# Two layers in fp32 on one core: the last expert slot's rows go to their tokens by a permutation product instead of through memory

## The chip, the cores and the metric

The kernel is written in Bass, with queues and semaphores set by hand, and runs on one core of one Trainium2 chip. The metric is the device time of one execution in microseconds, the median of several runs.

## What is computed

Eight tiles of 128 tokens, 256 wide (`x`, 1024 rows), go through two layers in fp32. Layer 0 is a cross attention with 16 heads of 16 and then a routed feed-forward with 8 experts; layer 1 is a cross attention with normed queries and keys, then a causal self attention of 16 heads of 128 and a second mixture of experts. This case concerns the passage from layer 0's experts to layer 1's cross attention:

```python
# layer 0, feed-forward: each token goes to its best expert only
route = sigmoid(h @ router_w); max_ind = argmax(route, 1); max_prob = its value
for e in range(8):
    out = out + where(max_ind == e, (silu(h @ gate_w[e]) * (h @ up_w[e])) @ down_w[e], 0)
x = x + tanh(g_ffn[0]) * out * max_prob
# layer 1, cross attention; its keys and values come from the context, not from x
q = rms_norm(layernorm(x) @ q_w.T + q_b) * norm_q_w
k = rms_norm(ctx @ k_img_w.T + k_img_b) * norm_k_img_w
v = ctx @ v_img_w.T + v_img_b
x = x + tanh(g_xattn[1]) * (attention(q, k, v) @ o_w.T + o_b)
```

## The kernel before, in words

**Slots.** The tokens are sorted by expert. `place` and `posf`/`pos` hold for each token its row in a list of 15 slots of 128 rows (`SLOTS`); a slot belongs to one expert. GpSimd scatters the normalised rows to `xs_d` in memory at these places (L1740), and each engine runs `slots`, which calls its `tile(j, ...)` for j = 0 to 14. In a slot TensorE turns the rows (L1453), makes gate and up products in three parts of split precision (`up`, L1461 to L1467), turns the hidden rows of the slot before (L1474) and multiplies them by the down weights (L1482). VectorE copies the result to `y_s` (`output_rows`, L1680), and SP stores it to `ys_d` (`store`, L1781).

**The passage.** When all 15 stores have landed, GpSimd gathers the rows of tile b back from `ys_d` into `FX` (eight indirect DMAs, L1765), and VectorE adds them to `X`, scaled by `rmax` (`add_experts`, L1604), and takes statistics (L1605, `moments` L841 to L843). GpSimd raises the variance to the power -1/2 (`power`, L800); VectorE makes the first two normalised tiles `xn` (`ln_scale`, L846). TensorE turns them (L453), ScalarE copies them to `xT` (`columns`, L671), TensorE makes the queries (L465), ScalarE their scaled form `qT` and squares (L689, L690), and then scores follow (L500).

**What stands beside it.** Keys and values of layer 1 are made from the context: `keys_values(i)` on TensorE (L1426) and VectorE (L1666, L1667, L783), six tiles early and the last two (`MOST` to `B`) after the last slot. `normalise_keys` (L1598) scales them. Each normalised key tile in `K1` is turned on TensorE (L1523) and copied back by ScalarE (`key_columns`, L1537). ScalarE makes the masked form `k2T` for the first two tiles (L711) and loads the table for Exp (L715); GpSimd makes it for the others (`masked_keys`, L984). `fill` (L347) issues products of zeros. SP then loads the first weights of the self attention (L2090, L2094) once the last down product is done.

**The attention's steps.** `xattn_*(.., 1)` runs steps n = -3 to 8. VectorE's step n has the two halves of softmax of tile n + 1 (`softmax`, L864 and L865, 128 by 1024 each), the mean of queries (L874), and the normalisation of the context of tile n (L869, L870), which TensorE turns in the next step (L453 on `x_cx`). At n = -1 stands `rest_of_rows()`. The order on every engine is the order of the calls; an engine waits at an instruction for its semaphores, with all that is behind it.

Constants: `B` 8, `EARLY` 4, `MOST` 6, `FIRST` 2. `KEYS` is [4, 5, 6, 7, 0, 1, 2, 3], the order in which key tiles are made.

## Time and profile before

| | us |
|---|---|
| median of 3 runs (lowest, highest) | 761.36 (760.95, 764.85) |
| profiled execution, its own time | 763.18 |
| its span, first to last instruction | 761.5 |
| TensorE busy | 728.8 |
| VectorE, ScalarE, GpSimd busy | 455.1, 374.2, 297.0 |
| chain that ended last: TensorE's share | 81% |
| mean granted clock of TensorE | 0.988 |

The span is cut up by what the engines do: layer 0's cross attention to about 87 us, its routing and slots to 189, the passage to about 206, layer 1's cross attention to about 282, then self attention and the second mixture.
### The profile page before, as it was taken

To read this page: it belongs to the slowest core of one execution; us is meant where nothing else is said; L and a number is where in the kernel's file an instruction comes from. 1 tells how busy PE (TensorE), PEld (TensorE's weight loads), DVE (VectorE), ACT (ScalarE), POOL (GpSimd) and SP (SyncE) were. 2 spreads that over 40 slices of the span, in tenths; PEclk is the share of its full clock that TensorE was granted. 3 is DMA by queue.
4 is the path that set the end of the run, shared out by engine and by line. 5 is a ranking of instruction groups with operands and counts; after the bars stand their busy time and mean duration, and the time that the engine had idled before them with its cause. 6 is when DMAs were issued, how large, how long until landed. Compare 5 with 4: busy or idle time off the path is not lost.

```text
span 761.5 us, 14062 instructions
## 1 busy us (share of the span) xinstructions
PE 728.8 (96%) x4683; PEld 611.3 (80%) x4684; DVE 455.1 (60%) x823; ACT 374.2 (49%) x876; POOL 297.0 (39%) x376
## 2 busy tenths in 40 slices
PE   7999989999889989999999999999999999999998
PEld 6887657887567767898899988998778888888886
DVE  6888587554687854345444554355555665665665
ACT  4888236664377754445445454445442323323323
POOL 3233265664655656422232123212324434434430
PEclk9999999999799999999999999999999999999999
DMA  8980121111300011010110101200004343343321
GB/s 286 418 329 2 28 83 36 55 41 35 118 2 1 2 36 36 22 35 22 36 55 21 34 21 46 72 1 22 22 25 129 114 121 100 121 116 99 122 95 56
DMA packets 24745, 57.40 MB, mean 75 GB/s; under 512 B 3568, under 2 KB 13296, under 8 KB 23680
## 3 DMA queue, kind: packets, MB, share of 16 engines
q1 hardware_dynamic: 23936, 54.77, 22.0%
q0 software_dynamic: 768, 2.10, 0.9%
q8 instruction: 25, 0.41, 0.2%
q14 instruction: 16, 0.13, 0.1%
HBM read 50.76 MB, written 6.09 MB: 75 GB/s over the span
## 4 chain that ended last, share of the span: by engine, by line
PE 81%; DVE 7%; ACT 6%; POOL 2%; DMA 2%; issue 1%; DVEq 0%; SPq 0%; ACTq 0%; POOLq 0%
PE PS L351 16%; PE PS L353 16%; PE PS L352 16%; PE PS L1824 7%; PE PS L1482 4%; PE PS L465 3%; PE PS L500 2%; PE PS L509 2%; PE PS L471 2%; PE PS L1830 2%; PE PS L1467 2%; PE PS L1464 2%; PE PS L1461 2%; PE PS L522 1%; POOL Z L846 1%
## 5 line engine op out<-in xcount | busy, mean ns | idle before, releaser
L1250 ACT ACTIVATE hhh<-hh 128x512 fp32r<-128x512 f32 x50 | 31.6, 632 | 104.6 <-DVE hh L1276 94.7
L351 PE MATMUL PS<-tTh,wh 128*128 128x512 f32 x200 | 78.3, 392 | 0.8 <-DVE tTl L661 0.5
L353 PE MATMUL PS<-tTh,wl 128*128 128x512 f32 x200 | 77.9, 389 | 0.0
L352 PE MATMUL PS<-tTl,wh 128*128 128x512 f32 x200 | 77.8, 389 | 0.0
L661 DVE TENSOR_TENSOR hhl<-hh,hhh 128x512 fp32r<-128x512 f32 x50 | 52.3, 1047 | 35.4 <-ACT hhh L1250 35.4
L1342 POOL CAST wh<-wraw 128x512 fp32r<-128x512 f32 (+1 forms) x50 | 26.1, 523 | 109.9 <-PE PS L353 109.9
L2038 POOL CAST ah<-araw 128x512 fp32r<-128x512 f32 (+1 forms) x32 | 16.2, 506 | 134.6 <-PE PS L353 134.6
L1935 ACT ACTIVATE sm<-sm,nmx 128x128 f32<-128x128 f32 x128 | 49.7, 390 | 37.7 <-DVE nmx L1998 37.7
L661 DVE TENSOR_TENSOR oTl<-PS,oTh 128x512 fp32r<-128x512 f32 x32 | 22.1, 691 | 71.5 <-ACT oTh L1929 71.5
L1344 POOL TENSOR_TENSOR wl<-wraw,wh 128x512 fp32r<-128x512 f32 (+1 forms) x50 | 58.0, 1160 | 8.4 <-POOL wh L1342 7.9
L1531 POOL TENSOR_TENSOR wgl<-WE,wgh 128x512 fp32r<-128x512 f32 x28 | 46.9, 1696 | 26.4 <-ACT wgh L1577 25.8
L351 PE MATMUL PS<-tTh,ah 128*128 128x512 f32 x128 | 53.0, 414 | 1.7 <-DVE tTl L834 1.5
L1272 DVE TENSOR_TENSOR act_s<-act_s,PS 128x512 f32<-128x512 f32 x44 | 30.2, 687 | 38.4 <-PE PS L353 38.4
L353 PE MATMUL PS<-tTh,al 128*128 128x512 f32 x128 | 50.2, 393 | 0.0
L352 PE MATMUL PS<-tTl,ah 128*128 128x512 f32 x128 | 49.9, 390 | 0.0
L1239 ACT ACTIVATE act_s<-PS 128x512 f32<-128x512 f32 x50 | 29.9, 599 | 32.0 <-PE PS L353 32.0
L351 PEld LDWEIGHTS PS<-tTh,wh 128*128 128x128 f32 x200 | 37.5, 188 | 9.9 <-issue 1.1
L353 PEld LDWEIGHTS PS<-tTh,wl 128*128 128x128 f32 x200 | 37.5, 188 | 7.9
L352 PEld LDWEIGHTS PS<-tTl,wh 128*128 128x128 f32 x200 | 37.5, 188 | 7.5
L864 DVE TENSOR_REDUCE x_mx<-PS 128x8 f32<-128x1024 f32 x32 | 38.9, 1217 | 5.7 <-PE PS L500 5.7
L1929 ACT ACTIVATE pT<-PS 128x512 f32<-128x512 f32 x32 | 17.6, 596 | 49.7 <-PE PS L1830 49.6
L865 DVE TENSOR_TENSOR x_prob<-PS,x_mx 128x1024 f32<-128x1024 f32 x32 | 39.2, 1224 | 1.1
(276 smaller groups left out, 1985.4 us busy)
## 6 DMA issues: line engine op xcount, KB each, us to landing
WE<-moe SPq DMA_DIRECT2D x8, 1536.0 KB, 18.1
wraw<-moe SPq DMA_DIRECT2D x25, 384.0 KB, 3.0
araw<-attn SPq DMA_DIRECT2D x16, 384.0 KB
cwb<-cw_d SPq DMA_DIRECT2D x20, 256.0 KB, 3.9
WX<-wx SPq DMA_DIRECT2D x4, 512.0 KB, 7.2
avraw<-attn_v SPq DMA_DIRECT2D x8, 256.0 KB
xs_d<-zeros SPq DMA_DIRECT2D x1, 1920.0 KB, 22.2
ys_d<-y_s SPq DMA_DIRECT2D x15, 128.0 KB, 1.7
```

The costliest lines, as they stand in the source:

```text
L351: nc.tensor.matmul(out, wh_, xh_, start=first, stop=False, **kw)
L352: nc.tensor.matmul(out, wh_, xl_, start=False, stop=False, **kw)
L353: return nc.tensor.matmul(out, wl_, xh_, start=False, stop=last, **kw)
L661: return nc.vector.tensor_tensor(lo, src, hi.bitcast(F32), ALU.subtract)
L864: ch.link(nc.vector.tensor_reduce(m8, sc, AX.X, ALU.max))
L865: nc.vector.tensor_tensor(m_.prob[b % 2][:, 8 * g:8 * g + 8, :], sc, m8.unsqueeze(2).broadcast_to([P, 8, S]), ALU.subtract).then_inc(s.sub ...
L1250: nc.scalar.activation(hhh[half][:, :], hh[half][:, :], ACT.Copy).then_inc(s.hi_done, 1)
L1344: nc.gpsimd.tensor_tensor(wl[par][:, a0:a1], wraw[par][:, a0:a1], wh[par][:, a0:a1].bitcast(F32), ALU.subtract).then_inc(s.w_split, 1)
L1482: m = nc.tensor.matmul(PS[:, 6 + par, 0:D], hT[:, k, :], w[:, k, :], start=(k == 0), stop=(k == I0 // P - 1))
L1531: eng.tensor_tensor(wgl[mat][:, c, :], expert_columns(e, mat, c), wgh[mat][:, c, :].bitcast(F32), ALU.subtract).then_inc(done, 1)
L1824: m = nc.tensor.matmul(PS[:, si % 4, t * S:(t + 1) * S], lhs[:, a0:a0 + S], rhs[:, a0:a0 + S], start=True, stop=True)
L1935: nc.scalar.activation(sm[:, b, :], sm[:, b, :], ACT.Exp, bias=nmx[:, b:b + 1], scale=AD ** -0.5, accum_out=sums[:, b:b + 1]).then_inc(aex ...
```

## The change

Slot 14's rows no longer go through memory. `ys_d`'s last slot is filled with zeros at the start, SP no longer stores slot 14, and GpSimd's gathers wait for slots 0 to 13 alone. For the tokens in slot 14 a permutation is made: SP writes the positions `posf` to `pos_d` in memory and reads them back to all partitions into `last_perm`, the free half of `rT`; one VectorE operation after slot 2 compares them with the rows of the last slot. TensorE multiplies `y_s[0]` by it for each tile (`last_product`) and adds the gathered rows of tiles 0 to 3 by a product with the identity in the same PSUM bank (`gathered_rows`). For tiles 4 to 7 ScalarE copies the product to `last_rows`, the space of `gs`, and VectorE adds it and the gathered rows one after the other, two tiles in step n = -1 and two in step n = 0. The key tiles are turned back in another order and in other banks (`TURNED`, `TURN_BANKS`), the last two (`LATE_KEYS`) in the attention's step n = -1; the fillers are fewer.

```diff
+LATE_KEYS = KEYS[B - 2:]
+TURNED = [4, 5, 0, 1, 2, 3]
+TURN_BANKS = [1, 3, 0, 2, 7, 6]
...
+        last_perm = rT[:, :, (B - CTX) * S:]
+        last_rows = gs2[:, :, :].rearrange("p a (k d) -> p (a k) d", d=D)
...
             # scores(b) on TensorE
+                if L and b == 0:
+                    pe.wait_ge(Es.k1_ready, 2)
+                    pe.wait_ge(Es.last_read, 2)
...
-            pe.wait_ge(Es.kt_free, B)
-            fill(4, 7)
+            pe.wait_ge(Es.kt_free, len(TURNED))
+            fill(2, 7)
...
+                if n == -1:
+                    pe.wait_ge(Es.k1_ready, 2)
+                    for b in LATE_KEYS:
+                        rows_to_columns("KT", b, K1[:, b, :])
...
-                key_columns(act, MOST, B)
...
-                if n == -1:
-                    rest_of_rows()
+                if n in (-1, 0):
+                    rest_of_rows(EARLY + 2 * n + 2)
...
+            def keys_back(k):
+                i, out = TURNED[k], PS[:, TURN_BANKS[k], :]
+                pe.wait_ge(s.k1_ready, 1)
+                for c in range(C):
+                    m = nc.tensor.transpose(out[:, c * P:(c + 1) * P], K1[:, KEYS[i], c * P:(c + 1) * P], ident[:, :])
+                m.then_inc(s.kt_done, 1)
+            def last_product(b, signal=False):
+                if b in FIRST_OF_BANK:
+                    pe.wait_ge(s.kt_free, FIRST_OF_BANK.index(b) + 1)
+                m = nc.tensor.matmul(last_bank(b), last_perm[:, b // EARLY, b % EARLY * P:(b % EARLY + 1) * P], y_s[0][:, :], start=(b in FIRST_OF_BANK), stop=signal, skip_group_check=True)
+                if signal:
+                    m.then_inc(s.last_done, 1)
+            def gathered_rows(b):
+                pe.wait_ge(s.gathered[b], 16)
+                if b >= FIRST:
+                    pe.wait_ge(s.place_read, b)
+                nc.tensor.matmul(last_bank(b), ident[:, :], FX[:, b, :], start=False, stop=True, skip_group_check=True).then_inc(s.last_done, 1)
             turn_hidden(SLOTS - 1)
+            keys_back(0)
+            keys_back(1)
             down(SLOTS - 1, (SLOTS - 1) % 2)
+            keys_back(2)
+            keys_back(3)
+            pe.wait_ge(s.perm_done, 2)
+            pe.wait_ge(s.y_ready, SLOTS)
+            for b in (0, 2, 1, 3):
+                last_product(b)
+            gathered_rows(0)
+            gathered_rows(1)
             for i in range(MOST, B):
                 keys_values(i)
-            for i in range(B):
-                if i == MOST:
-                    pe.wait_ge(s.kt_free, 3)
-                    fill(15, 2)
...
+            for b in range(EARLY, B):
+                last_product(b, b % 2 == 1)
+            keys_back(4)
+            keys_back(5)
+            gathered_rows(2)
+            gathered_rows(3)
...
             hidden_columns(SLOTS - 1)
-            key_columns(act, 0, MOST)
+            key_columns(act, 0, EARLY)
+            for k in range(2):
+                act.wait_ge(s.last_done, 3 + k)
+                nc.scalar.activation(gs2[:, k, :], PS[:, TURN_BANKS[2 + k], :], ACT.Copy).then_inc(s.last_read, 1)
+            key_columns(act, EARLY, len(TURNED))
...
             # add_experts(dve, ch, b); add(src) is the old operation with another source
+            if b < EARLY:
+                dve.wait_ge(Es.last_done, b + 1 if b < FIRST else b + 3)
+                add(last_bank(b)).then_inc(Es.place_read, 1)
+            else:
+                dve.wait_ge(Es.last_read, 2)
+                ch.link(add(last_rows[:, b - EARLY, :]))
+                dve.wait_ge(Es.gathered[b], 16)
+                ch.link(add(FX[:, b, :]))
...
+                if isinstance(j, int) and j == 2:
+                    dve.wait_ge(late_in, 64 + 16 * C)
+                    v.tensor_scalar(last_perm, last_perm, rows_after[:, :], float(SLOTS * P - 1), ALU.add, ALU.is_equal).then_inc(s.perm_done, 1)
...
             output_rows(SLOTS - 1, (SLOTS - 1) % 2, (SLOTS - 1) // 2)
+            for b in range(FIRST):
+                add_experts(dve, ch, b)
+            moments(ch, 0, FIRST)
             dve.wait_ge(s.kms_done, 1)
-            keys_values(MOST, B)
+            keys_values(MOST, MOST + 1, False)
+            powered(dve, "ln3")
+            for k in range(FIRST):
+                ln_scale(xb1.xn[k][:, :], X[:, k, :], k).then_inc(xs[1].ln_done, 1)
+            keys_values(MOST + 1, B)
+            for b in range(FIRST, EARLY):
+                add_experts(dve, ch, b)
+            moments(ch, FIRST, EARLY)
+            normalise_keys(dve, MOST, B, 2)
...
             for par in range(2):
-                pool.wait_ge(s.y_out[par], 16 * ((SLOTS + 1 - par) // 2))
+                pool.wait_ge(s.y_out[par], 16 * ((SLOTS - par) // 2))
             for b in range(B):
                 nc.gpsimd.indirect_dma_start(FX[:, b, :], None, ys_d, bass.IndirectOffsetOnAxis(pos[:, b:b + 1], 0)).then_inc(s.gathered[b], 16)
...
+                if b == MOST - 1:
                     power(pool, "ln3")
...
+            sp.dma_start(pos_d.rearrange("b p -> p b"), posf[:, :], allow_slow_non_contiguous=True).then_inc(late_in, 16)
+            sp.wait_ge(late_in, 64)
+            for c in range(C):
+                sp.dma_start(last_perm[:, c, :], pos_d[EARLY * c:EARLY * (c + 1), :].rearrange("b p -> (b p)").partition_broadcast(P)).then_inc(late_in, 16)
...
-            store(SLOTS - 1, (SLOTS - 1) % 2)
```

TensorE, from the last product of slot 14 (`WE,hT`) to the first scores, before (`WX,rT` are the last keys and values, `ident,K` the key transposes, `zeros` the fillers, `x_xn` the first normalised rows):

```order
L1482 MATMUL PS<-WE,hT 128x256
L1426 MATMUL PS<-WX,rT 128x512 x4
L1523 MATMUL PS<-ident,K 128x128 x12
L347 MATMUL PS<-zeros 128x512 x15
L1523 MATMUL PS<-ident,K 128x128 x4
L347 MATMUL PS<-zeros 128x512 x4
L453 MATMUL PS<-ident,x_xn 128x128 x2
L465 MATMUL PS<-x_xT,WX 128x128 x4
```

and with the change (`y_s,rT` is the product with the permutation, `FX,ident` the gathered rows):

```order
L1508 MATMUL PS<-WE,hT 128x256
L1540 MATMUL PS<-ident,K 128x128 x4
L1547 MATMUL PS<-y_s,rT 128x256 x4
L1557 MATMUL PS<-FX,ident 128x256 x2
L1452 MATMUL PS<-WX,rT 128x512 x4
L1547 MATMUL PS<-y_s,rT 128x256 x4
L1540 MATMUL PS<-ident,K 128x128 x4
L1557 MATMUL PS<-FX,ident 128x256 x2
L358 MATMUL PS<-zeros 128x512 x2
L464 MATMUL PS<-ident,x_xn 128x128 x2
L476 MATMUL PS<-x_xT,WX 128x128 x4
```

The keys and values of the last two tiles now stand behind six products, two of which wait for gathers.

ScalarE in the same place, before (`warm` is the one element that carries the table load):

```order
L1550 ACTIVATE hT<-PS 128x512 [waits e_ht_done] x2
L1537 ACTIVATE K<-PS 128x256 [waits e_kt_done] x6
L711 ACTIVATE x_k2T<-K,pair_rows 128x2x128 [waits e_kt_free,bias_done]
L711 ACTIVATE x_k2T<-K,pair_rows 128x2x128
L711 ACTIVATE x_k2T<-K,pair_rows 128x2x128 [waits e_kt_free]
L711 ACTIVATE x_k2T<-K,pair_rows 128x2x128
L1537 ACTIVATE K<-PS 128x256 [waits e_kt_done] x2
L715 ACT_TABLE_LOAD
L715 ACTIVATE warm<-mhalf 128x1
L671 ACTIVATE x_xT<-PS 128x256 [waits x1_turn_done]
```

and with the change:

```order
L1611 ACTIVATE hT<-PS 128x512 [waits e_ht_done] x2
L1598 ACTIVATE K<-PS 128x256 [waits e_kt_done] x4
L1651 ACTIVATE gs<-PS 128x512 [waits e_last_done] x2
L1598 ACTIVATE K<-PS 128x256 [waits e_kt_done] x2
L730 ACTIVATE x_k2T<-K,pair_rows 128x2x128 [waits e_kt_free,bias_done]
L730 ACTIVATE x_k2T<-K,pair_rows 128x2x128
L730 ACTIVATE x_k2T<-K,pair_rows 128x2x128 [waits e_kt_free]
L730 ACTIVATE x_k2T<-K,pair_rows 128x2x128
L733 ACT_TABLE_LOAD
L733 ACTIVATE warm<-mhalf 128x1
L690 ACTIVATE x_xT<-PS 128x256 [waits x1_turn_done]
```

The masked key tiles (`x_k2T`) stand behind two copies `gs<-PS` that wait for the products with the permutation, and the table load stands behind them.

VectorE with the change, from the first softmax to the second (`x_mx<-PS`, `x_prob` are one half of it):

```order
L885 TENSOR_REDUCE x_mx<-PS 128x8 [waits x1_scores_done]
L886 TENSOR_TENSOR x_prob<-PS,x_mx 128x1024 [waits dve_chain]
L1669 SCALAR_TENSOR_TENSOR X<-gs,rmax,X 128x256 [waits e_last_read]
L1669 SCALAR_TENSOR_TENSOR X<-FX,rmax,X 128x256 [waits e_gathered4,dve_chain]
L1680 BN_STATS st<-X 128x6 [waits dve_chain]
L1669 SCALAR_TENSOR_TENSOR X<-gs,rmax,X 128x256 [waits e_last_read]
L1669 SCALAR_TENSOR_TENSOR X<-FX,rmax,X 128x256 [waits e_gathered5,dve_chain]
L1680 BN_STATS st<-X 128x6 [waits dve_chain]
L862 BN_AGGR mv<-st 128x2 [waits dve_chain]
L862 BN_AGGR mv<-st 128x2
L864 TENSOR_SCALAR ms<-mv 128x2 [waits dve_chain]
L895 TENSOR_SCALAR q_mean<-PS 128x1 [waits x1_turn_done]
```

Before, this place had one addition (tile 7), its statistics and the moments of four tiles; the same seven rows of additions now stand after the second softmax as well.

## Rows read from the trace of the kernel before

**Rows 1.** The page, busy time of the engines (share of the span, instructions):

```profile
PE 728.8 (96%) x4683; PEld 611.3 (80%) x4684; DVE 455.1 (60%) x823; ACT 374.2 (49%) x876; POOL 297.0 (39%) x376
```

**Rows 2.** Chain of waits in order of time (start us, us, what), between the layers:

```profile
189.19 0.43 DVE y_s L1680
189.65 1.71 DMA ys_d<-y_s
191.63 4.15 DMA FX<-ys_d,pos
...
202.15 0.39 ACT x_xT L671
```

**Rows 3.** Timeline of TensorE (start us, us, line, what, count of records [idle before]):

```profile
87.99 3.26 PE L1426 MATMUL PS<-WX,x_cT 128*128 128x512 f32 x4
...
187.17 1.99 PE L1482 MATMUL PS<-WE,hT 128*128 x8 [0.79 <-ACT hT L1550]
188.99 3.60 PE L1426 MATMUL PS<-WX,rT 128*128 128x512 f32 x8
192.43 1.63 PE L1523 MATMUL PS<-ident,K 128*128 128x128 f32 x12
...
202.59 2.07 PE L465 MATMUL PS<-x_xT,WX 128*128 128x128 f32 x8 [0.47 <-ACT x_xT L671]
...
223.33 0.38 PE L453 MATMUL PS<-ident,x_cx 128*128 128x128 f32 x2
```

**Rows 4.** Timeline of ScalarE in the same stretch:

```profile
186.42 0.60 ACT L1550 ACTIVATE hT<-PS 128x512 f32<-128x512 f32 x1 [3.07 <-PE PS L1474]
...
194.44 1.74 ACT L711 ACTIVATE x_k2T<-K,pair_rows 128x256 f32<-128x256 f32 x4
199.39 0.66 ACT L1537 ACTIVATE K<-PS 128x256 f32<-128x256 f32 x2 [3.21 <-PE PS L1523]
200.07 1.28 ACT L715 ACT_TABLE_LOAD   x1
201.37 0.20 ACT L715 ACTIVATE warm<-mhalf 128x1 f32<-128x1 f32 x1
```

**Rows 5.** Stretches: us, busy by engine, granted clock, DMA share, GB/s:

```profile
192.00:194.00 2.00, 2.00 (x15) 1.50 (x14) 1.19 (x6) 1.16 (x5) 1.62 (x2) 1.00 1.02 355
...
202.00:204.00 2.00, 1.53 (x7) 1.41 (x7) 1.54 (x4) 0.38 (x1) 1.52 (x3) 0.50 0.24 66
```

**Rows 6.** Timeline of VectorE, end of the slots and first steps of attention:

```profile
185.98 0.42 DVE L1680 COPY y_s<-PS 128x256 f32<-128x256 f32 x1 [1.20 <-PE PS L1482]
...
200.96 0.73 DVE L846 TENSOR_SCALAR x_xn<-X,mv,rstd 128x256 f32<-128x256 f32 x2
...
213.05 0.47 DVE L1604 SCALAR_TENSOR_TENSOR X<-FX,rmax,X 128x256 f32<-128x256 f32 x1
...
214.51 0.15 DVE L874 TENSOR_SCALAR q_mean<-PS 128x1 f32<-128x1 f32 x1
...
220.62 0.16 DVE L874 TENSOR_SCALAR q_mean<-PS 128x1 f32<-128x1 f32 x1 [1.18 <-PE PS L488]
221.37 0.26 DVE L869 RECIPROCAL x_rden<-PS 128x16 f32<-128x16 f32 x1 [0.59 <-PE PS L529]
221.66 0.42 DVE L870 TENSOR_TENSOR x_cx<-PS,x_rden 128x256 f32<-128x256 f32 x1
```

**Rows 7.** GpSimd's timeline, second gather, and the gathers' landing (their line's view):

```profile
192.97 0.96 POOL L1765 DMA_INDIRECT FX<-ys_d,pos  x1 [0.30 <-issue]
...
DMA to landing us min/median/max: 2.7/2.8/2.8
```

**Rows 8.** VectorE's permutation, a load's landing, and SP's loads of slot rows:

```profile
94.66 1.22 DVE L1652 TENSOR_TENSOR gs<-PS,posf 128x1024 f32<-128x1024 f32 x1
...
rw<-rw SPq DMA_DIRECT2D x1, 16.0 KB, 6.5
...
L1777 SPq DMA_DIRECT2D xs_s<-xs_d x5: 327/340/425, 107.8 to 124.7; - x5
```

More of the change, by code:

```diff
@@ L170, in build @@
         pos = sb("pos", [P, B], mybir.dt.uint32, e)
+        rows_after = sb("rows_after", [P, 1], where=e)
+        last_perm = rT[:, :, (B - CTX) * S:]
+        last_rows = gs2[:, :, :].rearrange("p a (k d) -> p (a k) d", d=D)
         exf = sb("exf", [P, SLOTS], where=e)
@@ L316, in build @@
             xt_done, xt_ready, g_done, u_done, silu_done = (sem("e_" + k) for k in ("xt_done", "xt_ready", "g_done", "u_done", "silu_done"))
[L317 removed]
+            place_read, perm_done, h_ready, ht_done, ht_ready, d_done, y_ready = (sem("e_" + k) for k in ("place_read", "perm_done", "h_ready", "ht_done", "ht_ready", "d_done", "y_ready"))
             xt_low, w_high = sem("e_xt_low"), sem("e_w_high")
             w_low = [sem(f"e_w_low{i}") for i in range(2)]
+            last_done, last_read = sem("e_last_done"), sem("e_last_read")
             sums_done, experts_done, zeroed = sem("e_sums_done"), sem("e_experts_done"), sem("e_zeroed")
@@ L392, in second_turns @@
                     ("xT", n + 3, "A"), *(("F", b, "D") for b in ins), ("O", n - 1, "D"), ("oT", n, "A"),
-                    *([("Q2", n + 2, "D")] if n > -2 else []), ("cx", n, "D"),
+                    *([("Q2", n + 2, "D")] if n > -2 else []), ("cx", n, "D"), *([("KT", b, "A") for b in LATE_KEYS] if n == -1 else []),
                     *(("F", b, "D") for b in {B - 1: [4], B: [5, 6, 7]}.get(n, []))]
@@ L767, in xattn_act @@
                     columns("xT", n + 3, m_.xT)
+                if n == -1:
+                    for b in LATE_KEYS:
+                        copy("KT", b, K1[:, b, :], D)
                 if B - 4 <= n < B:
@@ L788, in build @@
         X_PARTS = [(0, FIRST), (FIRST, EARLY), (EARLY, B)]
-        POWERS = [("ln1", 0, FIRST), ("ln1", FIRST, EARLY), *(("ln1", b, b + 1) for b in range(EARLY, B)), ("ln2", 0, EARLY), ("ln2", EARLY, MOST), ("ln2", MOST, MOST + 1), ("ln2", MOST + 1, B), ("ln3", 0, FIRST), ("ln3", FIRST, EARLY), ("ln3", EARLY, B),
+        POWERS = [("ln1", 0, FIRST), ("ln1", FIRST, EARLY), *(("ln1", b, b + 1) for b in range(EARLY, B)), ("ln2", 0, EARLY), ("ln2", EARLY, MOST), ("ln2", MOST, MOST + 1), ("ln2", MOST + 1, B), ("ln3", 0, FIRST), ("ln3", FIRST, EARLY), ("ln3", EARLY, MOST), ("ln3", MOST, B),
                   ("ln4", 0, B)]
@@ L1006, in xattn_pool @@
                     routing_constants()
-                if L and n == 1:
-                    power(pool, "ln3", EARLY)
+                if L and n in (1, 3):
+                    power(pool, "ln3", EARLY + n - 1)
                 if n + 3 < B:
@@ L1427, in keys_values @@
                 m.then_inc(s.kv_done, 1)
-            nc.tensor.matmul(PS[:, 6, 0:P], ones[:, :], earlier[:, :], start=True, stop=True).then_inc(s.ids_done, 1)
+            nc.tensor.matmul(PS[:, 6, 0:P], ones[:, :], earlier[:, :], start=True, stop=True).then_inc(s.lg_done, 1)
             pe.wait_ge(wx_in[1][0], 16)
@@ L1513, in ffn_pe @@
+            pe.wait_ge(s.y_ready, SLOTS)
[3 more added lines that the diff above has]
+            gathered_rows(1)
             for i in range(MOST, B):
                 keys_values(i)
-            for i in range(B):
-                if i == MOST:
-                    pe.wait_ge(s.kt_free, 3)
-                    fill(15, 2)
-                pe.wait_ge(s.k1_ready, 1 if i < MOST else 2)
-                after(pe, s.kt_free, i - 3)
-                for c in range(C):
-                    m = nc.tensor.transpose(PS[:, i % 4, c * P:(c + 1) * P], K1[:, KEYS[i], c * P:(c + 1) * P], ident[:, :])
-                m.then_inc(s.kt_done, 1)
+            for b in range(EARLY, B):
+                last_product(b, b % 2 == 1)
@@ L1526, in expert_columns, with last_bank @@
+            keys_back(4)
+            keys_back(5)
+            gathered_rows(2)
+            gathered_rows(3)
+        FIRST_OF_BANK = [0, 1, EARLY, MOST]
+        def last_bank(b):
+            k, part = (b % FIRST, b // FIRST) if b < EARLY else (b // 2, b % 2)
+            return PS[:, TURN_BANKS[k], part * D:(part + 1) * D]
         def expert_columns(e, mat, c):
@@ L1619, in ffn_dve @@
             ch.link(v.memset(V1[:, :, :, XD:XD + 1], 1.0))
+            v.tensor_reduce(rows_after[:, :], earlier[:, :], AX.X, ALU.add)
             dve.wait_ge(s.ex_done, 1)
@@ L2213, in _, with more_rows @@
             ffn_dve(dve, ch)
-            for b in range(B - 1):
-                add_experts(dve, ch, b)
-                if b == FIRST - 1:
-                    moments(ch, 0, FIRST)
-                    normalise_keys(dve, MOST, B, 2)
-                if b == EARLY - 1:
-                    moments(ch, FIRST, EARLY)
-                    powered(dve, "ln3")
-                    for k in range(FIRST):
-                        ln_scale(xb1.xn[k][:, :], X[:, k, :], k).then_inc(xs[1].ln_done, 1)
-            def last_rows():
-                add_experts(dve, ch, B - 1)
-                moments(ch, EARLY, B)
-            xattn_dve(dve, 1, ch, last_rows)
+            def more_rows(b0):
+                for b in range(b0, b0 + 2):
+                    add_experts(dve, ch, b)
+                moments(ch, b0, b0 + 2)
+            xattn_dve(dve, 1, ch, more_rows)
             attn_dve(dve, ch)
```

31 lines of the change are left out of this document (17 added, 14 removed).

## The prediction

> **What bounds the kernel now.** I read the page's busy shares first: the reader sees TensorE busy 96% of the span [rows 1], so time is lost or won only where TensorE waits for others, above all between the two layers. There I followed the chain of waits: after the last expert slot's product VectorE copies the rows (189.19), they are stored (189.65, 1.71 us), read back by the first gather (191.63, landed 4.15 us later), and only 12.5 us after the store does ScalarE copy the first normalised rows of the new layer (202.15) [rows 2]. TensorE's own timeline shows what it does meanwhile: the last two key and value products at once (188.99 to 192.43), then twelve key transposes, then fillers [rows 3]. ScalarE's timeline shows that two masked key tiles and the table load were out of the way in that wait [rows 4]. Two stretches give the transfers' load and the clock: 1.00 until the gathers, 0.50 (the lower level, 1.2 GHz) at 202 to 204 [rows 5]. VectorE's timeline gives the additions and the first steps of the attention after [rows 6].
>
> **Step 1, the gathers start sooner.** They waited for slot 14's store, and now for slot 13's. The copies of these rows end at 186.40 (185.98 + 0.42 [rows 6]) and 189.61 [rows 2], so the first gather starts 3.2 us sooner, at 188.4, the second 1.34 us after it as before [rows 2, 7], at 189.8. Landing is bounded by 2.8 us (the usual one [rows 7]) and 4.15 us (the first gather of before [rows 2]). That one shared the DMA engines with the loads of attention weights, which fill them (share 1.02 at 192 to 194 [rows 5]). SP no longer holds these loads behind the last store, so they are issued about 0.7 us sooner, and the second gather falls among them. I take 3.7 us, nearer the loaded row: the second gather lands at 193.5 (bounds 192.6 and 193.9).
>
> **Step 2, TensorE's queue.** It does in order: two key transposes in the idle time before the down product (free, 0.8 us of wait stands there), two after it, then four products with the permutation. A product of 128 by 256 in fp32 costs 0.44 us (four, recorded as eight passes, 1.76 us apart from the next work, 187.17 to 188.95 [rows 3]); from 189.65 they end at 191.4. Then it **waits for gathers 0 and 1 with the last key and value products queued behind**: its identity product of 0.44 us ends at 193.95, where before these K and V products stood at 188.99. So 5.0 us of cover is gone. K and V take 3.44 us (188.99 to 192.43 [rows 3]), the four other products with the permutation 1.76 us: 199.15.
>
> **Step 3, ScalarE's queue.** It has two copies of 128 by 512 that wait for those products, then two key copies, then the two masked key tiles, then the table load, then the first transposed rows. The second large copy starts at 199.3; 0.48 us (the 0.60 us of such a copy less its overlap [rows 4]) gives 199.8, two key copies 0.68 us (199.39 to 200.07), masked tiles 1.74 us, table and warming 1.50 us (200.07 to 201.57 [rows 4]): 203.7. Before, that copy began at 202.15 [rows 2]: **1.55 us later**, although the rows it wants are ready sooner. Those rows: adds at 194.0, statistics at 195.4, powers after the sixth gather on GpSimd at 196.6, normalised rows at 197.1 instead of 200.96 [rows 6]. That gain of 3.9 us is lost in this queue. The table load is 1.28 us in the row, with 0.20 us of warming behind it. The Trainium skill (ScalarE: Activation LUTs, What ACT_TABLE_LOAD costs) states the same 1.28 us but adds a drain of 1.38 us, 2.66 us in all, and by it the queue would end 1.2 us later still; no such gap stands between load and warming here, so the row decides and the rule gets no chance of its own.
>
> TensorE idles in this wait, from about 201.5 to 204.1, so I expect the lower clock again. The first two query products took 2.07 us together at that level [rows 3]; four passes of K and V took 3.26 us at it and 1.72 us (half of 188.99 to 192.43) at the full one, so about 1.1 us of the 2.07 would do. The fall comes later against the work than before, and I take 0.35 us of that 1.0 as given back: the first scores are 1.2 us late.
>
> **Step 4, VectorE between softmaxes.** The rows of tiles 4 to 6 were added in idle time before the first scores, tile 7 in 1.46 us after softmax 0 (213.05 to 214.51 [rows 6]). Now tiles 4 and 5 stand after softmax 0 and 6 and 7 after softmax 1, each with two additions (one for the product, one for the gather). Per tile: 0.51 + 0.51 + 0.37 us; for two with their moments 3.2 us. The first pair costs 3.2 - 1.46 = 1.75 us. Of the second, VectorE's waits before the normalisation (1.18 and 0.59 us [rows 6]) hide 1.8: 1.4 us. So the first normalised context, which ended at 222.08 (221.66 + 0.42 [rows 6]), ends 1.2 + 1.75 + 1.4 = 4.35 us later, at 226.4. TensorE wanted it at 223.33 [rows 3]: **3.1 us late**. From there TensorE is the bound again, as in the rest of the span [rows 1], so I count nothing as won back.
>
> **What hides.** The permutation's preparation: positions stored as 1024 pieces of four bytes, spread over the partitions by two loads, and one operation on 128 by 1024. The last is some 1.2 us like the other comparison of that size [rows 8], after slot 2 on VectorE, which waits for TensorE in each slot. The store is bounded by 1.7 us (a plain store [rows 2]) and 6.5 us (the router weights, 16 KB in short pieces [rows 8]); with 4 us for the loads all ends before 107, and SP next has work at 107.8 [rows 8]. Cost 0, for either bound. The Trainium skill (DMA: Bandwidth & Descriptors, Specifications) says that writes below 512 B become read-modify-write; that speaks for the upper bound, and no row shows such a store. The sum of this reduces to nothing as long as the store lands within 12 us. The row sum over 128 columns is 0.2 us before a wait for TensorE, the extra zero tile 128 KB beside 1920. The two late key transposes with their copies lie in the first steps, where TensorE waits for ScalarE anyway, and the fillers that go were idle time.
>
> **Sum.** 3.1 us on the profiled execution's 763.18 us is 766.3. That execution is 1.82 us above the median of the runs shown, so I forecast **764.5 us**. About 0.5% (3.8 us) is what a measurement of this kernel tells from no change.
>
> **Rivals.**
> - *The clock falls in the wait for the gathers* (slower). TensorE has only transposes and small products from 191.4 to 193.5, and the K and V products follow. For: 0.50 was granted after the thin stretch before 202. Against: this wait is shorter, 2 us, and broken by a product. Four passes of them took 3.26 us at the lower level [rows 3], so eight cost up to 3.1 us more, 1.7 us if half run so: 766.2 to 767.6. It decides as soon as the granted clock in 194 to 197 is below 1. Chance 0.2.
> - *The gathers do not come sooner in effect*: all land late among the weight loads, 4.15 us each and more. +0.5 to +1 us on the forecast, 765.3. Chance 0.1.
> - *The adds are covered* and only step 3 costs: the pair after softmax 1 is hidden and the second gather lands after 2.8 us. 764.5 less 1.4 and 0.9 is 762.2. Chance 0.2.
> - *The 3.9 us gained at the first normalised rows pass through* (faster). It needs ScalarE free at 198.3 and TensorE fed, with the clock kept: 761.4 less 3.9, 757.5. For: the chain of before runs exactly there. Against: the table load and masked tiles are queued behind the products in program order. Chance 0.1.
> - *The positions come late*, so that the change brings nothing but its costs: a store over 12 us holds SP's load of slot 1 and from there TensorE, by the excess; at 16 us 4 us more, 768.5. Chance 0.03.
>
> **How the numbers follow.** The forecast itself has 0.37: 763 to 766 with gather and clock bounds, so about half of its upper part crosses 765.2. Slower: 0.2 + 0.05 + 0.03 + 0.12 = 0.40. Faster: 0.1. Same: 0.50. The range from 760.5 (the covered case less the clock kept in the first steps, 1 to 2 us) to 768.0 (the clock case at its bound) leaves out the faster case, the last rival and a little of the others.
>
> **What would show it.** Step 1: first gather at 188.4. Step 2: the K and V products at about 194, at clock 1.00. Step 3: the two masked key tiles and the table load directly before the first transposed rows at 203.7, with these rows' normalisation finished 5 us earlier. Step 4: two runs of four additions after softmax 0 and 1, 3.2 us each. I am wrong if the table load is over before 201, if TensorE does not wait between 201 and 204, or if the first context is not late at 226.

## The result, and the profile after

| | before | after |
|---|---|---|
| median (range) of 4 runs each | 761.94 us (760.95 to 764.85) | 773.12 us (770.43 to 774.12) |
| ratio, 95% interval | | 1.0142 (1.0113 to 1.0170) |
| profiled execution: span, clock | 761.5 us, 0.988 | 772.4 us, 0.986 |

The change makes the kernel 11 us slower; 764.5 was forecast, 768.0 was the upper end of the range. The page's busy line answers to [rows 1]: TensorE works 3.7 us more, the span is 10.9 us longer. The chain has a new entry.

```profile
PE 732.5 (95%) x4690; PEld 612.3 (79%) x4691; DVE 457.6 (59%) x830; ACT 375.3 (49%) x878; POOL 297.0 (38%) x377
...
PE 79%; DVE 8%; ACT 6%; POOL 2%; issue 2%; DMA 1%; another core or an unknown queue 1%; SPq 0%; ACTq 0%; DVEq 0%; POOLq 0%
```

Two landmarks show where the 10.9 us are lost, both in VectorE's timeline: the copy y_s of slot 14's rows, and the first normalised context x_cx. The first moved from 189.19 [rows 2] to 195.75, so **6.6 us are lost before the slots end**. From it to x_cx it was 32.5 us (221.66 [rows 6]) and is 39.3: **6.8 us between the layers**. Of these 13.4 us the attention gives 2.5 back by its last context (281.06 before, 291.94 after).

```profile
195.75 0.42 DVE L1756 COPY y_s<-PS 128x256 f32<-128x256 f32 x1 [2.79 <-PE PS L1508]
...
223.41 0.47 DVE L1669 SCALAR_TENSOR_TENSOR X<-gs,rmax,X 128x256 f32<-128x256 f32 x1
223.92 0.48 DVE L1669 SCALAR_TENSOR_TENSOR X<-FX,rmax,X 128x256 f32<-128x256 f32 x1
...
231.48 0.48 DVE L1669 SCALAR_TENSOR_TENSOR X<-gs,rmax,X 128x256 f32<-128x256 f32 x1
231.99 0.48 DVE L1669 SCALAR_TENSOR_TENSOR X<-FX,rmax,X 128x256 f32<-128x256 f32 x1
...
235.05 0.42 DVE L891 TENSOR_TENSOR x_cx<-PS,x_rden 128x256 f32<-128x256 f32 x1
```

**Before the slots.** The chain of waits, where the first slot starts: ScalarE loads its table and then waits 8.19 us for something that the profile cannot name; only then comes the first gate copy (the Silu of slot 0's gate products, `gs`), which before stood at 104.47. It is not the gate products that it waits for: TensorE ended them at 105.26 in after, 5.8 us ahead of the copy, but at 104.43 in before, right ahead of it.

```profile
101.55 1.28 ACT L1616
102.83 8.19 another core or an unknown queue
111.02 0.02 issue
111.04 0.61 ACT gs L1616
```

What is new in this place is the store of the positions. SP's timeline: issued at 95.58, and SP, which waits for its landing, issues the spreading loads at 107.02, so it took up to 11.4 us.

```profile
95.58 0.37 SPq L1885 DMA_DIRECT2D pos_d<-posf  x1
107.02 1.15 SPq L1888 DMA_DIRECT2D rT<-pos_d  x2
110.97 0.81 SPq L1866 DMA_DIRECT2D xs_s<-xs_d  x2
```

The DMA queues in that stretch, 95 to 112 us (packets, MB, share of 16 engines' time), of after (`software_dynamic` carries GpSimd's scatters):

```profile
DMA packets 1695, 1.55 MB, mean 91 GB/s; under 512 B 1193, under 2 KB 1205, under 8 KB 1694
...
q0 software_dynamic: 384, 1.05, 52.2%
```

And of before:

```profile
DMA packets 673, 1.32 MB, mean 78 GB/s; under 512 B 160, under 2 KB 416, under 8 KB 672
...
q0 software_dynamic: 384, 1.05, 17.6%
```

The same 384 packets of GpSimd's scatters hold the engines for three times as long.

**Between the layers.** GpSimd issues the first gather 0.86 us behind the landing of slot 13's rows (194.68 in the chain of waits), 0.27 us in before:

```profile
195.54 1.04 POOL L1856 DMA_INDIRECT FX<-ys_d,pos  x1 [6.50 <-DMA ys_d<-y_s]
```

TensorE's timeline, to be read beside [rows 3]:

```profile
193.72 1.99 PE L1508 MATMUL PS<-WE,hT 128*128 x8 [0.35 <-ACT hT L1611]
...
196.27 1.97 PE L1547 MATMUL PS<-y_s,rT 128*128 128x256 f32 x8
200.26 0.70 PE L1557 MATMUL PS<-FX,ident 128*128 128x256 f32 x2 [2.02 <-DMA FX<-ys_d,pos]
201.70 1.07 PE L1557 MATMUL PS<-FX,ident 128*128 128x256 f32 x2 [0.74 <-DMA FX<-ys_d,pos]
202.56 4.97 PE L1452 MATMUL PS<-WX,rT 128*128 128x512 f32 x8
207.36 1.89 PE L1547 MATMUL PS<-y_s,rT 128*128 128x256 f32 x8
...
213.85 1.16 PE L476 MATMUL PS<-x_xT,WX 128*128 128x128 f32 x8 [2.34 <-ACT x_xT L690]
...
235.53 0.44 PE L464 MATMUL PS<-ident,x_cx 128*128 128x128 f32 x2 [0.89 <-DVE x_cx L891]
```

It waits 2.02 and 0.74 us for the two gathers, then does the last K and V products in 4.97 us where [rows 3] has 3.60. The granted clock says why (columns as in [rows 5]): it fell to 0.50 in that very stretch, behind one in which TensorE was busy for 0.24 us of 2.

```profile
198.00:200.00 2.00, 0.24 (x2) 0.00 (x0) 0.00 (x0) 0.00 (x0) 1.54 (x2) 1.00 1.03 388
202.00:204.00 2.00, 2.00 (x4) 1.06 (x4) 1.13 (x4) 0.00 (x0) 0.85 (x1) 0.50 0.41 117
```

ScalarE's queue behind it, as [rows 4]: 11.8 us idle, then everything at once.

```profile
208.43 0.60 ACT L1651 ACTIVATE gs<-PS 128x512 f32<-128x512 f32 x1 [11.80 <-PE PS L1547]
209.29 0.60 ACT L1651 ACTIVATE gs<-PS 128x512 f32<-128x512 f32 x1 [0.27 <-PE PS L1547]
209.78 0.66 ACT L1598 ACTIVATE K<-PS 128x256 f32<-128x256 f32 x2
210.31 1.70 ACT L730 ACTIVATE x_k2T<-K,pair_rows 128x256 f32<-128x256 f32 x4
212.03 1.28 ACT L733 ACT_TABLE_LOAD   x1
213.33 0.20 ACT L733 ACTIVATE warm<-mhalf 128x1 f32<-128x1 f32 x1
213.44 0.36 ACT L690 ACTIVATE x_xT<-PS 128x256 f32<-128x256 f32 x1
```

### The profile page after: what moved, and what is told of

It reads as the page before. It is cut to its first block, busy times and chain, and to the rows that moved or that the text cites. A ratio compares the mean times of both kernels' runs of the same rounds, so it can differ in the third digit from the quotient of the medians.

```text
span 772.4 us, 14093 instructions
## 1 busy us (share of the span) xinstructions
PE 732.5 (95%) x4690; PEld 612.3 (79%) x4691; DVE 457.6 (59%) x830; ACT 375.3 (49%) x878; POOL 297.0 (38%) x377
## 4 chain that ended last, share of the span: by engine, by line
PE 79%; DVE 8%; ACT 6%; POOL 2%; issue 2%; DMA 1%; another core or an unknown queue 1%; SPq 0%; ACTq 0%; DVEq 0%; POOLq 0%
PE PS L362 16%; PE PS L364 15%; PE PS L363 15%; PE PS L1917 7%; PE PS L1508 3%; PE PS L476 2%; PE PS L482 2%; PE PS L515 2%; PE PS L524 2%; PE PS L1923 2%; PE PS L1493 2%; PE PS L1487 2%; PE PS L1490 2%; PE PS L1452 1%; PE PS L537 1%
## 5 line engine op out<-in xcount | busy, mean ns | idle before, releaser
L2022 ACT ACTIVATE pT<-PS 128x512 f32<-128x512 f32 x32 | 17.6, 596 | 49.7 <-PE PS L1923 49.6
```

## The experiments

The runs carry the names of the table. The ratio of each is to runs of the kernel before on the same chip; four chips were used, on which before took 761.9 to 762.9 us, so runs of different groups are compared by their ratios. "Gap" is from slot 14's y_s to the first x_cx in the run's profile, one execution; in the seven profiles of before and of versions of it, it is 30.4 to 33.4 us, mean 31.5: 30.4 to 31.9 in the four where the granted clock was 1.00 from 186 to 212 us, 32.5 and 33.4 in the two where it was 0.80. "Gate" is the start of ScalarE's first gate copy.

| run | us | ratio (95%) | gate | y_s | gap |
|---|---|---|---|---|---|
| before | 761.94 | 1 | 104.47 | 189.19 | 32.5 |
| after | 773.12 | 1.0142 (1.0113, 1.0170) | 111.04 | 195.75 | 39.3 |
| e1_before_pos | 765.93 | 1.0046 (1.0025, 1.0067) | 109.77 | 192.78 | 31.3 |
| e2_after_nopos | 767.46 | 1.0049 (1.0027, 1.0071) | 102.16 | 186.89 | 39.3 |
| e3_before_store | 766.38 | 1.0044 (1.0024, 1.0064) | 109.81 | 194.54 | 30.5 |
| e4_before_loads | 761.58 | 0.9985 (0.9961, 1.0009) | 105.04 | 189.78 | 31.9 |
| e12_store_rows | 762.01 | 0.9999 (0.9977, 1.0021) | 103.64 | 188.51 | 30.4 |
| e15_store_late | 761.11 | 0.9982 (0.9964, 1.0000) | 104.93 | 189.71 | 30.9 |
| e18_after_store_late | 767.83 | 1.0094 (1.0060, 1.0127) | 103.22 | 188.06 | 37.4 |
| e13_after_again | 770.48 | 1.0140 (1.0103, 1.0178) | 106.66 | 191.22 | 39.1 |
| e5_pe_positions | 770.18 | 1.0103 (1.0072, 1.0134) | 106.27 | 189.19 | 40.5 |
| e6_kv_first | 765.48 | 1.0055 (1.0035, 1.0075) | 106.83 | 189.69 | 35.1 |
| e7_act_order | 765.48 | 1.0041 (1.0018, 1.0064) | 108.55 | 191.42 | 34.8 |
| e14_loads_later_alone | 765.80 | 1.0042 (1.0026, 1.0059) | 106.02 | 189.85 | 36.5 |
| e8_both | 764.55 | 1.0030 (1.0015, 1.0045) | 105.25 | 188.15 | 33.5 |
| e9_adds | 762.29 | 1.0014 (0.9991, 1.0036) | 105.32 | 190.16 | 32.6 |
| e10_loads_later | 761.76 | 0.9996 (0.9978, 1.0013) | 104.42 | 188.62 | 32.7 |
| e11_best | 761.05 | 0.9989 (0.9967, 1.0011) | 103.43 | 187.90 | 29.5 |
| e17_best_store_late | 762.34 | 1.0016 (0.9988, 1.0043) | 102.68 | 187.44 | 31.5 |
| e16_before_loads_later | 764.58 | 1.0032 (1.0015, 1.0050) | 102.52 | 187.36 | 33.4 |

### Who loses the time before the slots

e1 puts the new transfers, and nothing else, into the kernel before (line L1794, SP):

```diff
+            sp.wait_ge(s.pos_done, 1)
+            sp.dma_start(pos_d.rearrange("b p -> p b"), posf[:, :], allow_slow_non_contiguous=True).then_inc(late_in, 16)
+            sp.wait_ge(late_in, 64)
+            for c in range(C):
+                sp.dma_start(rT[:, c, (B - CTX) * S:], pos_d[EARLY * c:EARLY * (c + 1), :].rearrange("b p -> (b p)").partition_broadcast(P)).then_inc(late_in, 16)
             sp.wait_ge(s.scattered, 16 * B)
```

> The kernel before plus the store of the 1024 positions and the two loads that spread them; nothing reads what they load. Theory P (the positions' way through memory costs about 6 us in the expert slots: the profile of after has ScalarE's first gate copy 8.21 us late and the last down product 6.55 us later than before): 766 to 769 us, with ScalarE idle some 8 us ahead of its first gate copy. Rival C (the slots are late in after because TensorE's clock fell at another place, by chance or through the changed tail's placement): within 1 us of before, 762.

e2 takes them out of after (the comparison then waits for `late_in` at 48). e3 adds only the store and its wait to before, e4 only the two loads, from `vec_d[0:EARLY * P]`.

> The kernel after without that store and those loads: the permutation is made from whatever lies in its place, so the last slot's rows reach no right token. Theory P: 6 us faster than after, 766 to 768 us, with the last down product back near 187 to 188. Rival C: as after, 773.

> The kernel before plus only the store of the positions (1024 pieces of 4 bytes). If the small pieces are what delays the others: 4 to 7 us slower than before (766 to 769) and ScalarE's first gate copy late. If it is the 256 KB x 2 of spread loads that collide with the scatters: within 1 us of before.

> The kernel before plus only the two loads that spread 512 numbers over the partitions, issued as the positions are ready, reading an input in the place of the positions (same size and pieces). If the small pieces of the store are the cause: within 1 us of before, 762. If the loads are: 3 to 6 us slower, 765 to 768.

The store alone costs what store and loads cost, and the loads nothing that can be measured. e3's chain of waits has the long wait of after (first below); in e4 ScalarE's gate copy waits 2.45 us, as in before (second).

```profile
100.76 1.28 ACT L1556
102.05 7.74 another core or an unknown queue
...
109.81 0.61 ACT gs L1556
```

```profile
101.30 1.28 ACT L1556 ACT_TABLE_LOAD   x1
105.04 0.60 ACT L1556 ACTIVATE gs<-PS 128x512 f32<-128x512 f32 x1 [2.45 <-issue]
```

The gate copy is 5.3 us late in e3, the total 3.4 us: part comes back, as the gap of 30.5 shows (at a granted clock of 1.00 there, where before had 0.80).

e12, against e3, stores the same 4 KB there as 8 pieces of 512 B:

```diff
-            sp.dma_start(pos_d.rearrange("b p -> p b"), posf[:, :], allow_slow_non_contiguous=True).then_inc(late_in, 16)
+            sp.dma_start(pos_d, earlier[0:B, :]).then_inc(late_in, 16)
```

e15 issues e3's store later, in SP's slot body:

```diff
                     store(j - 1, 1 - par)
+                if is_second(j):
+                    sp.dma_start(pos_d.rearrange("b p -> p b"), posf[:, :], allow_slow_non_contiguous=True).then_inc(late_in, 16)
```

> The kernel before plus one store of the same 4 KB at the same place, but as 8 pieces of 512 B and not 1024 of 4 B (of an array of the same size, not of the positions). If the number of pieces is what costs: as before, 762, the first gate copy not late. If any store there costs (its wait, its place in the queue): 766 as with the small pieces.

> The kernel before plus the same store of 1024 pieces of 4 B, issued some 17 us later, in slot 1, when the scatters have landed and ScalarE runs in its loop. If it costs by what was in flight at its old place: 762 to 763. If it costs wherever it stands (slot loads and stores behind it on the same 16 engines, 11 us long): 765 to 767.

Neither costs anything that can be measured. In e12 the scatters hold 17.6% of the engines' time from 95 to 112 us, as in before, in e3 51.0%. In e15 the small pieces do slow what is beside them: the load of a slot's rows that shares the queues with them lands after 6.5 us, in before after 2.0, but no engine is held up by it.

```profile
xs_s<-xs_d SPq DMA_DIRECT2D x1, 128.0 KB, 6.5
pos_d<-posf SPq DMA_DIRECT2D x1, 4.0 KB, 8.0
```

So neither a store there nor small pieces cost by themselves; the small pieces cost **while the scatters and what ScalarE waits for are in flight**. e15 also leaves out SP's wait for the landing. That wait is no rival: in after SP is through with it at 107.02 and issues the slot loads only at 110.97. e18 moves the store so in after itself (store in slot 1, loads in slot 13, comparison in the last slot) and e13 is after once more:

> The kernel after with only this moved: store of the positions in slot 1, the two spread loads in slot 13, the comparison behind that slot's rows on VectorE. If the store's place is worth 3 to 4 us, as adding it to before says: 768 to 769.5. If it is worth the 5.7 us of the run without positions: 766.5 to 767.5.

> The kernel after, unchanged, beside the three others of this group: 771 to 774 us, 1.2 to 1.5% over before. If the split of the variants (store 3.4, tail 7 to 8) is right, 772.5.

1.0142 and 1.0140 against 1.0094: the store's place is worth 0.47%, 3.6 us. e13 (770.48) lies 0.5 us under its forecast, e15 (761.11) 0.9 under, e1 (765.93) at the lower edge of its own. The intervals of 1.0142, 1.0140 and 1.0094 leave anything from 0.1 to 0.9%, so e18 (767.83, between its two forecasts) does not decide between them; the tighter figure is e3's own 3.4 us (0.24 to 0.64%), and the two agree. e2 is 0.93%, 7 us, below after, more than the store. In its profile the clock stayed at 1.00 ahead of the slots, where that of before fell (first K/V products 1.88 us in e2, 3.26 in [rows 3]); but that is one execution, and why e2 lies below e18, with the same work between the layers, is not shown. Their intervals overlap.

### Who loses the time between the layers

The rest is 0.94% (7.2 us) by e18 and 0.49% (3.7 us) by e2. By the profiles it lies between the layers: both gaps are 6 to 8 us longer than the mean of before. e5 is the base of what follows: positions spread by TensorE instead of through memory.

```diff
+            for c in range(C):
+                for b in range(EARLY):
+                    m = nc.tensor.matmul(PS[:, 4 + 2 * c, b * P:(b + 1) * P], posf[:, EARLY * c + b:EARLY * c + b + 1].broadcast_to([P, P]), ident[:, :], start=True, stop=True)
+                m.then_inc(s.last_read, 1)
             keys_values(3)
...
             columns(0, 0)
+            for c in range(C):
+                act.wait_ge(s.last_read, C)
+                nc.scalar.activation(last_perm[:, c, :], PS[:, 4 + 2 * c, :], ACT.Copy).then_inc(s.last_read, 1)
             slots(act, tile)
```

> The kernel after, whole, but the positions are spread over the partitions by eight TensorE products (a column of positions, spread, times the identity) and two ScalarE copies, ahead of the slots, and no longer through memory. If the store of 4-byte pieces is the one cause of the slots' delay: 766 to 768 us as without positions (5 to 7 under after), ScalarE's first gate copy back near 2.5 us of waiting. If the products and copies take ScalarE's slack (2.45 us there, 1.2 us of copies): up to 1 us more.

770.18 is a miss (766 to 768 was expected, and its 1.0103 is no better than e18): the copies push the table load to 103.00, and the gate copy, with 1.98 us of a wait that the profile cannot name, to 106.27. Its gap, 40.5, holds K and V products of 6.00 us. Three edits follow, each alone on e5: e6 on TensorE, e7 on ScalarE (`masked_keys` is L724 to L733, taken from their place), e14 on SP ahead of the next stage's loads; e8 has the first two.

```diff
                 last_product(b)
+            for i in range(MOST, B):
+                keys_values(i)
             gathered_rows(0)
             gathered_rows(1)
-            for i in range(MOST, B):
-                keys_values(i)
...
             key_columns(act, 0, EARLY)
+            masked_keys(act)
             for k in range(2):
                 act.wait_ge(s.last_done, 3 + k)
...
-            sp.wait_ge(Es.d_done, SLOTS)
+            sp.wait_ge(Es.gathered[1], 16)
```

> As the run with TensorE's positions, and K/V 6 and 7 (L1452) stand ahead of the first two gathered rows on TensorE, so that it works while the gathers fly. Theory (TensorE idle under the gathers and then at the lower clock delays what ScalarE waits for, last_done 3 and 4): the eight K/V products take 3.6 us at full clock and not 5, the copies that block ScalarE start 3.5 to 5 us sooner, the first cx turn 3 us sooner; 763 to 764.5 us. Rival (the gathered rows, now 1.6 us later, are what DVE's chain to x_xn waits for): within 1 us of the run with TensorE's positions.

> As the run with TensorE's positions, and ScalarE makes the masked keys 0 and 1 and its table load while it waits, ahead of the two copies of the last rows (L1651). Theory (ScalarE's queue is what holds x_xT): x_xT 3.2 us sooner, 763.5 to 765 us. Rival (x_xT waits for x_xn or TensorE anyway): within 1 us of the run with TensorE's positions.

> After with TensorE's positions, and the only other edit is that the next stage's weight loads wait for the second gather. Theory (they hold up the first gathers by 1.5 us, and TensorE idles and falls to the lower clock for it): gathers land after 2.8 us, TensorE waits under 0.5 us for each, 766 to 768.5 us (770.2 without the edit). Rival (TensorE's clock falls there anyway, or ScalarE's queue hides it): 769.5 to 771.

> Both reorderings on TensorE's positions. If the two causes add: 759 to 761.5 us, at or under the kernel before. If both stand in one chain and the longer hides the other: 763 to 764. If even then the adds of the last four token blocks (3.2 us twice on DVE) hold the first cx turn: 762 to 763, with the turn waiting for DVE x_cx.

By the ratios e6, e7 and e14 take 0.48, 0.62 and 0.61% off e5 (3.7 to 4.7 us), e6 and e7 together 0.73% (5.6 us), less than their sum; the gaps say the same, 5.4 and 5.7 us shorter alone, 7.0 together. They work on **one chain** (gathers, K and V, last products, ScalarE's copies, table load, x_xT), so they do not add. The times alone would not prove it, since e5 has four executions. e6, e7 and e8 came out 1.0, 0.5 and 0.6 us above their forecasts for this case (to 764.5, to 765, to 764), e14 0.2 us below its own. In e7's profile x_xT no longer waits behind the table load; of its shorter gap, though, 2.4 us are K and V at the full clock (3.60 us), which is not the edit's: e18 has the same 3.60 us without it.

```profile
193.90 1.28 ACT L1601 ACT_TABLE_LOAD   x1
...
202.41 0.60 ACT L1658 ACTIVATE gs<-PS 128x512 f32<-128x512 f32 x1 [7.01 <-PE PS L1542]
...
205.58 0.39 ACT L690 ACTIVATE x_xT<-PS 128x256 f32<-128x256 f32 x1 [1.17 <-PE PS L464]
```

e14 shows that the gathers were slow because of the loads beside them. In e5 they are issued at 189.19, right behind the first gather at 189.00, in e14 at 193.79, 4.1 us behind it (189.65). There TensorE waits 0.68 us for the second gather alone, where e5 waited 1.50 and 1.40 us, and K and V keep the clock.

```profile
192.43 0.70 PE L1561 MATMUL PS<-FX,ident 128*128 128x256 f32 x2
193.82 0.70 PE L1561 MATMUL PS<-FX,ident 128*128 128x256 f32 x2 [0.68 <-DMA FX<-ys_d,pos]
194.35 3.60 PE L1452 MATMUL PS<-WX,rT 128*128 128x512 f32 x8
```

e9 adds to e8 that VectorE's additions of tiles 4 and 5 stand ahead of the attention's loop, those of 6 and 7 in its steps 1 and 2; e10 adds e14's edit to e8 and puts only K/V 6 first, two things at once; e11 has both e9 and e10.

```diff
+            more_rows(EARLY)
             xattn_dve(dve, 1, ch, more_rows)
...
-                if n in (-1, 0):
-                    rest_of_rows(EARLY + 2 * n + 2)
+                if n in (1, 2):
+                    rest_of_rows(MOST + n - 1)
```

> As the run with both reorderings, and DVE's adds of token blocks 4 and 5 stand ahead of the second attention's loop, where DVE waits 2.58 us for the first scores, those of 6 and 7 one each in steps 1 and 2, where its slack is 1.4 us in 8.4. Theory (the two runs of adds, 3.2 us each, stand in the chain from x_xT to the first x_cx): the first x_cx 4 to 5 us sooner than in the run with both, of which the later steps keep 2 to 3; 761 to 762.5 us. Rival (the chain to the first x_cx is given back in the loop anyway, whose period of 8.4 us TensorE sets): within 1 us of the run with both, 764.5.

> As the run with both reorderings, but the loads of the next stage's weights (0.9 MB, issued beside the gathers) wait until the second gather has landed, and only K/V 6 stands ahead of the first gathered rows, K/V 7 behind them. Theory (these loads are why the first gathers take 4.2 to 4.7 us and not the 2.7 to 2.8 of the others): the first gather lands within 3 us of its issue, x_xn 1 to 1.5 us sooner than with both; 763 to 764. Rival (the first gathers are slow by themselves): they land after 4.2 us as before, TensorE waits for them and its clock may fall; 765 to 767.

> The two edits together, the best version that the theories give: 759.5 to 762 us, within 0.4% of the kernel before on either side. If it is still 1 us or more above before, what the change adds elsewhere (the last products, 3.9 us of TensorE) is worth its gain.

e11 is level with before (0.9989, and 1 lies in the interval). So is e10 already (0.9996, 1.2 us better than its forecast), and the timed runs do not tell e9 from e8 or e11 from e10: what the additions cost is seen in the gaps alone. e11's first context comes 29.5 us after y_s. e17 tried to win the rest with the store in its free place, and e16 whether the later loads help the kernel before:

> All remedies, and the positions go through memory again, stored in slot 1, where that cost nothing, and spread in slot 13. TensorE's products and ScalarE's copies of the positions fall away, which delayed the first gate copy by 1.8 us (106.27 against 104.47). If that is what kept the best version level with before: 758.5 to 760, faster than before by 0.3 to 0.5%. If not: 761 to 762 as the run with the best of both.

> The kernel before with the next stage's weight loads behind its second gather. Its gathers are issued 0.7 us behind those loads and landed after 2.7 to 2.8 us, so they lose little: 761.5 to 762.5, no change. If they did cost it too: 760 to 761.

Neither came true. e17 (1.0016) is no better than e11: its gate copy comes at 102.68, e11's at 103.43, but its first query products ran slower, as the two timelines of TensorE show, e17's first. e16 is 0.3% slower than before, where no change was expected; its profile, of its fastest execution, shows a gap of 33.4 us at a granted clock of 0.80 in 186 to 212, the same as before's, and does not tell why. No version beats the kernel before.

```profile
200.05 1.70 PE L476 MATMUL PS<-x_xT,WX 128*128 128x128 f32 x8 [0.54 <-ACT x_xT L690]
```

```profile
199.58 1.16 PE L476 MATMUL PS<-x_xT,WX 128*128 128x128 f32 x8 [0.91 <-ACT x_xT L690]
```

## Why the prediction was wrong

- **"What hides. ... Cost 0, for either bound"** is the step that failed first: it measured 3.4 us (e3; 3.6 by e18, with a wide interval). In the profiles y_s came 6.0 us later at the router's lower clock (195.75 against 189.7 and 189.8 of e15 and e4) and 3.3 at the full one (e13's 191.2 against 187.4 and 188.5 of e16 and e12). The store took up to 11.4 us where the bounds were 1.7 and 6.5, taken from rows with far fewer pieces. The sum's own condition, "as long as the store lands within 12 us", held, and still the cost came: it asked only what SP does next (its loads wanted at 107.8) and not which other transfers share the engines. The scatters, 17.6% of the engines' time in the stretch before, took 52.2%, and ScalarE waited. The rival of late positions named the right part with the wrong mechanism, at 0.03. The store is not all: with it moved away e18 is still 0.94%, 7.2 us, over before, where 3.1 were forecast for everything. The other steps have to account for that.
- **The rule on writes below 512 B.** The Trainium skill (DMA: Bandwidth & Descriptors, Specifications) says that such a write becomes a read-modify-write. e3 and e12 agree in direction: 1024 pieces of 4 B cost 3.4 us, 8 of 512 B nothing; they change number and size together, so they do not show which of the two counts, nor whether anything is read and written back. e15 shows what the rule does not say: the same pieces slow the load beside them (6.5 us instead of 2.0) and are free when nothing waits for it.
- **Step 1** had the right sign and was too hopeful. Relative to slot 14's down product the first gather starts 2.6 us sooner (191.63 - 187.17 = 4.46 us behind it before, 195.54 - 193.72 = 1.82 after), not 3.2, since GpSimd issues it 0.86 us behind the store's landing and not 0.27. The gathers landed after 4.7 us (195.54 to 200.26), not 3.7. "Nearer the loaded row" was the right thought; the attention loads, now issued right behind the first gather, made them slower than that row.
- **Step 2** was right in the mechanism (K and V behind the gathers) and wrong in the forecast between its two cases: the rival "The clock falls in the wait for the gathers", 0.2, came true, at a little under its price of 1.7 to 3.1 us. The K and V products took 4.97 us (6.00 and 5.29 in e5 and e2, 3.60 in e18 and e7): 1.4 us here.
- **Step 3** is the term of the sum that was mis-sized: **1.55 us forecast, 4.7 measured**. The order held: two large copies, two keys, masked keys, table load, x_xT, with x_xn ready 5.5 us ahead of it (207.96 and 213.44). But x_xT stood 14.98 us behind the down product before (202.15 - 187.17) and 19.72 after (213.44 - 193.72). The lateness was there before the queue began: the second large copy was 3.4 us later than forecast. It stood 15.57 us behind the down product (209.29 - 193.72) where 12.1 was forecast (199.3 - 187.17), 1.65 us of the difference are the second gather (201.70, which is 195.15 on the scale of before, for 193.5), 1.5 us K and V.
- **The gain itself** was missed too: the first normalised rows were to come 3.9 us sooner and came 0.4 sooner (207.07 - 193.72 = 13.35 us behind the down product, 200.96 - 187.17 = 13.79 before). With the loads held back and K and V reordered (e11) they come 3.7 us sooner (195.95 - 185.87 = 10.08).
- **Step 4** held: two runs of four additions, 223.41 to 226.6 and 231.48 to 234.7, and TensorE waits for x_cx. Of the gap's 6.8 us, 4.7 are step 3's and 2.1 are left for these less what the clock gave back. 1.75 + 1.4 - 0.35 = 2.8 was said, but the first query products took 1.16 us at the full clock where [rows 3] has 2.07, so 0.9 came back and not 0.35. Moved out of the chain, the additions bring the gap from 33.5 to 32.6 (e9) and from 32.7 to 29.5 (e11); the first of these is within what one profile differs from the next.
- **"I count nothing as won back"** was wrong on the good side: the first period after x_cx is 7.28 us (242.33 - 235.05) where it was 8.39, and so in every version with the four additions there. The other 1.4 of the 2.5 us won back lie in the last step (7.17 us, 8.56 before) and are not the change's: e15, which leaves the attention as it was, has 7.18 there.
- The rival "the 3.9 us gained pass through" fell, for the reason given against it (the table load and the masked tiles stood behind the products). That was not all: with these obstacles gone too (e11) the gap is only 2.0 us under the mean of before and the time level with it.

**Open** is what ScalarE waits for. The queue that the profile calls "instruction" had one packet in this stretch in each profile, at 102.77 in before and at 107.46 in after, so it too was late. It comes 0.7 to 0.8 us behind the end of the table load in before, e4, e12 and e15, and 3.6 to 4.6 us behind it in after, e1, e3 and e13, which have the small pieces there; the gate copy follows it by 1.7 us in the former, where TensorE's products release it, and by 3.1 to 3.6 in the latter. But in e5 the packet comes at 101.61, ahead of the table load, and ScalarE still waits 1.98 us behind that load. No run tells whether ScalarE waits for this packet or for something else. Of after, 107.25 to 107.5:

```profile
q14 instruction: 1, 0.01, 8.3%
```

## What to carry to other kernels

A small transfer is to be costed by its pieces and by what else is in flight, not by its bytes or by who reads it: ask of every new store which scatters, gathers and fetches it meets, and put it where nothing is waited for (here, one slot later, free). When a wait between engines is shortened, look at the whole queue behind it: three obstacles in one chain (loads beside the gathers, work behind a wait, a table load behind copies) cost some 7 us, each removed alone seemed worth 4 to 5, and all removed only returned the kernel to where it was.

## What was not expected of the hardware

- A store of 4 KB in 1024 pieces of 4 B landed after up to 11.4 us, and an engine that has no part in it, ScalarE, stood idle for 6.8 to 8.2 us in the four versions that have it there, where the kernel before has 2.45; the same store 18.6 us later (113.42 in e15, 94.78 in e3) landed after 8.0 us and cost nothing in the total.
- ScalarE waits about 2 us behind the table load ahead of its slots, for something that the profile does not name, also in versions without a store there (1.98 to 2.01 us in e5, e6, e7 and e8); in e9 and e10, where the table load comes late enough, it does not wait at all (104.00 + 1.28, then 105.32 in e9). In before its 2.45 us there are TensorE's.
- The same products ahead of the slots, in the same order, ran at granted clocks of 0.76, 0.88 or 1.00 (86 to 100 us) in profiles of different versions, and y_s of slot 14 moved with it: 189.7 to 189.8 in e4 and e15 at 0.76, 187.4 and 188.5 in e16 and e12 at 1.00. One profile's landmark is good to some 2 us here, no better; the timed ratios decided.
